# A graph layer on one core: dense attention weights as relu(A*B - 1), written to PSUM by ScalarE, and rows left unscaled

## The chip, the core and the metric

The program runs on one core of a Trainium2 chip. A core has five engines that run their own instruction streams and meet at semaphores: PE (TensorE, matrix multiplications), DVE (VectorE), ACT (ScalarE), POOL (GpSimd, which here issues the gathers) and SP (SyncE, which issues the other DMAs). PSUM is the memory that PE writes to, in eight banks; SBUF is the large on-chip memory. The metric is the device time of one execution in microseconds (us); smaller is better.

## What is computed

The input is a graph of 6250 nodes with 128 features each and 100000 edges `src -> dst`, the edges sorted by `dst`. Low node numbers receive many more edges than high ones.

```python
hs, hd = h[src], h[dst]; e = concat([hs, hd], axis=1)
a_k   = exp(relu(e @ W_att_k + b_att_k))                 # three heads
att_k = segment_sum(a_k, dst)
avg_a = (a1 / att1[dst] + a2 / att2[dst] + a3 / att3[dst]) / 3.0
m     = avg_a * relu(relu(relu(hs @ W1 + b1) @ W2 + b2) @ W3 + b3)
deg   = segment_sum(1, dst)
h_neigh = segment_sum(m, dst) / max(deg, 1)
ref   = relu(concat([h, h_neigh]) @ W_c1 + b_c1) @ W_c2 + b_c2
out   = layernorm(x + ref)
```

The logit of an edge is a sum of a part of its source and a part of its target. With A the exponential of the source's part and B that of the target's (bias included), the factor of a head is `exp(relu(p + q)) = max(A*B, 1)`.

## The kernel before

The program first computes for all nodes, in blocks of 128, their message row and the logit parts, and stores rows of 131 values (128 of the message, 3 logits) in a table in HBM, `message_table`. Then comes the pass over the edges, `edge_pass`.

Edges are taken in groups of 256 (two tiles of 128). The 94 groups with the lowest targets, which all lie in the first 384 nodes, are the hot groups: their edges are not gathered. They are counted into a dense matrix `counts` of 6250 sources by 384 targets (steps 0 to 24), and later the messages of all sources, 49 blocks of 128, are multiplied with dense weights. That is the hot stage: block b is made in step 27 + b, so it fills the steps 27 to 75. The remaining 297 groups are cut into 126 units (four groups each up to unit 23, two after it), one unit a step. POOL gathers a unit's rows by indirect DMA, one for each tile of 128 edges (four a unit from unit 24 on; L1247), into a ring of 12 places. A place comes free when PE has used it, which is what `s_sum` tells.

What a step i does on each engine, in the order of its stream, with the names that the texts use:

- DVE: in the hot stage `hot_weights(b, 0)` (L1765); `logits_of(i + 1)`: a reduction (L1859) and the addition of the gathered logits (L1865), which is the instruction that waits for the gathers of unit i + 1; `weights(i + 1)`: a clamp of the exponentials (L1885) and the product with the one-hot mask (L1890), whose width grows with the unit, 384 elements for 32 columns up to 576 for 48; `hot_weights(b, 1)`, `hot_weights(b, 2)` (L1765); `add_sums(i - 1)`, two additions to the accumulator (L1907); then steps of the finals.
- ACT: `mask_copy(i + 1)` (L1604), `exps(i + 1)` (L1564), finals, `one_hot(i + 3)` (L1554 and L1556), and in the hot stage `scale_rows(b)`: three copies of the block's 129 columns, each times A of one head (L1543).
- PE: `add_edges(i)` (L1434 and L1440), `edge_q(i + 2)` (L1386), in the hot stage `hot_edges(b - 1)`, nine products of 129 columns (L1473, each shown as two instructions in the profile), then finals (L904 and others).

The weights of a head in the hot stage before: `hot_weights` takes `max(B, 1/A)` of the 384 targets (`hot_b` holds B on all lanes, `inverse` holds 1/A), times the counts, and `scale_rows` puts the missing factor A on the rows. Both are in SBUF and neither waits for the other; only PE waits for both.

After the hot stage (`hot_end`, step 77) the hot sums are added, and the finals begin: eleven chunks of four blocks of nodes and three small ones, each in eight steps, spread over the remaining steps to 125, and a tail after the last unit. The order of every stream is written out by hand in the loops over i, and each engine works its stream in order.

## Time and profile before

| | us |
|---|---|
| median of 3 runs (784.7 to 786.55) | 785.11 |
| the profiled execution | 788.37 |
| its span | 784.4 |
| PE busy | 635.0 (81%) |
| DVE busy | 562.6 (72%) |
| ACT busy | 460.2 (59%) |
| POOL busy | 573.6 (73%) |

The span goes from the first to the last instruction of the profiled execution; its own time is 4.0 us longer. Busy shares are means over stages with different limits. The views used below are the chain of waits (what released what, followed back from the end), the waits by engine and line, the timeline, windows (busy time in stretches) and the groups of instructions by shape.

### The profile page before, as it was taken

How to read it: one execution, taken by the hardware profiler on the slowest of the kernel's cores; microseconds unless marked ns; L12 is line 12 of the kernel's file. 1: busy time of each engine (PE TensorE's matmuls, PEld its weight loads, DVE VectorE, ACT ScalarE, POOL GpSimd, SP SyncE). 2: the span in 40 equal slices, each digit the busy share in tenths (PEclk: the TensorE clock that was granted, in tenths of full speed). 3: DMA queues.
4: the chain of work that ended last, by engine and by line, in shares of the span. 5: the costliest groups of instructions: out<-in, count | busy, mean ns of one | idle time of the engine just before them, and what ended most of it. 6: DMA issues, size and time to landing. Idle time of an engine off the chain costs nothing.

```text
span 784.4 us, 17056 instructions
## 1 busy us (share of the span) xinstructions
PE 635.0 (81%) x5157; PEld 519.2 (66%) x5157; DVE 562.6 (72%) x1855; ACT 460.2 (59%) x1109; POOL 573.6 (73%) x604
## 2 busy tenths in 40 slices
PE   9951889988878777999998788797778877878775
PEld 5741657764655456899988677685667766767664
DVE  4884587588888787788886666665567777677566
ACT  6566687578655455667765555553365556566533
POOL 7777777777777677777777777777777777777760
PEclk9985596599778776899999989988798988899698
DMA  7974263334862233333433333324344444444321
GB/s 228 252 195 105 66 101 84 71 85 78 69 83 75 54 96 80 83 87 87 88 83 80 78 74 83 73 64 133 66 107 104 104 111 128 104 117 104 89 59 35
DMA packets 83313, 75.69 MB, mean 96 GB/s; under 512 B 35064, under 2 KB 66720, under 8 KB 83216
## 3 DMA queue, kind: packets, MB, share of 16 engines
q0 software_dynamic: 19008, 39.82, 25.8%
q1 hardware_dynamic: 63920, 34.59, 16.3%
q8 instruction: 44, 0.72, 0.4%
q14 instruction: 53, 0.43, 0.2%
q10 hardware_dynamic: 288, 0.13, 0.1%
HBM read 64.94 MB, written 9.52 MB: 95 GB/s over the span
## 4 chain that ended last, share of the span: by engine, by line
PE 33%; POOL 30%; issue 13%; DVE 11%; ACT 6%; DMA 5%; DVEq 1%; SPq 0%; POOLq 0%; ACTq 0%
POOL work L1247 30%; PE bank L1434 8%; PE bank L1473 7%; PE bank L1457 4%; PE bank L1440 2%; DVE counts L1730 2%; ACT fin L1578 2%; DVE acc L1907 2%; PE bank L592 2%; PE bank L613 2%; PE bank L1391 1%; DVE fin L1717 1%; PE bank L601 1%; DMA message_table<-work 1%; PE bank L1419 1%
## 5 line engine op out<-in xcount | busy, mean ns | idle before, releaser
L1247 POOL DMA_INDIRECT work<-message_table,src_t x554 | 531.6, 960 | 174.2 <-issue 164.9
L1434 PE MATMUL bank<-work 128*128 128x144 f32 (+8 forms) x1188 | 188.5, 314 | 37.9 <-DVE acc L1907 37.8
L1434 PEld LDWEIGHTS bank<-work 128*128 128x128 f32 x1188 | 174.3, 223 | 50.8 <-issue 43.8
L1604 ACT COPY work<-bank 128x192 f32<-128x192 f32 (+7 forms) x126 | 37.4, 297 | 177.4 <-DVE work L1859 176.0
L1473 PE MATMUL bank<-shared,fin 128*128 128x129 f32 (+1 forms) x882 | 115.1, 286 | 0.0
L1907 DVE TENSOR_TENSOR acc<-acc,bank 128x192 f32 (+8 forms) x297 | 89.1, 300 | 27.4 <-issue 3.6
L1473 PEld LDWEIGHTS bank<-shared,fin 128*128 128x128 f32 (+1 forms) x882 | 106.1, 197 | 2.5 <-issue 0.6
L1890 DVE TENSOR_TENSOR work<-bank,work 128x576 f32<-128x576 f32 (+7 forms) x126 | 86.2, 684 | 13.1
L1765 DVE SCALAR_TENSOR_TENSOR fin<-logits_or_x,per_node,counts 128x384 f32<-128x384 f32 (+1 forms) x147 | 85.8, 611 | 1.9 <-PE bank L1473 1.9
L904 PE MATMUL bank<-rest_w,acc 128*128 128x128 f32 x294 | 52.3, 344 | 40.5 <-DVE fin L995 31.0
L904 PEld LDWEIGHTS bank<-rest_w,acc 128*128 128x128 f32 x294 | 46.5, 246 | 43.0 <-DVE fin L995 32.3
L1865 DVE TENSOR_TENSOR work<-work 128x12 f32<-128x12 f32 (+1 forms) x126 | 22.0, 175 | 73.1 <-DMA work<-message_table,src_t 63.8
L1556 ACT ACTIVATE side<-side,one_col 48x512 bf16<-48x512 bf16 x100 | 72.0, 720 | 3.2
L1554 ACT ACTIVATE side<-side,less_col 48x512 bf16<-48x512 bf16 x100 | 70.5, 705 | 0.0
L1457 PE MATMUL bank<-fin 128*128 128x294 bf16 (+2 forms) x188 | 51.4, 416 | 19.4 <-ACT fin L1583 15.8
L1440 PE MATMUL bank<-work 128*4 128x48 f32 (+8 forms) x1188 | 64.8, 204 | 0.0
L1730 DVE TENSOR_TENSOR counts<-counts,bank 128x294 f32 (+2 forms) x94 | 56.3, 599 | 8.2 <-issue 7.3
L1564 ACT ACTIVATE work<-work 128x12 f32<-128x12 f32 (+1 forms) x126 | 27.0, 214 | 55.4 <-DVE work L1865 54.2
L1578 ACT ACTIVATE fin<-fin 128x128 bf16<-128x128 f16 x188 | 59.3, 386 | 0.0
L1386 PE MATMUL bank<-side 48*128 48x57 bf16 (+8 forms) x594 | 37.1, 185 | 24.1 <-DMA side<-logit_parts 20.0
L1440 PEld LDWEIGHTS bank<-work 128*4 128x4 f32 x1188 | 46.0, 89 | 15.9 <-issue 3.4
L1717 DVE TENSOR_SCALAR fin<-fin 128x294 bf16<-128x294 f16 (+2 forms) x188 | 56.4, 343 | 0.0
(162 smaller groups left out, 840.4 us busy)
## 6 DMA issues: line engine op xcount, KB each, us to landing
work<-message_table,src_t POOLq DMA_INDIRECT x554
side<-near_nodes SPq DMA_DIRECT2D x102, 48.0 KB
side<-logit_parts SPq DMA_DIRECT2D x297, 0.8 KB
message_table<-work SPq DMA_DIRECT2D x12, 262.0 KB, 4.7
work<-message_table SPq DMA_DIRECT2D x48, 65.5 KB
work<-in_x_t SPq DMA_DIRECT2D x12, 256.0 KB, 4.9
fin<-in_x SPq DMA_DIRECT2D x11, 256.0 KB, 3.0
logits_or_x<-in_x_t SPq DMA_DIRECT2D x11, 256.0 KB, 3.7
```

The lines of the kernel that those rows point to most:

```text
L904: last = pe.matmul(to[:, k * P:(k + 1) * P], acc[:, k, nodes], wc1[:, 1, :], start=True, stop=True)
L1247: pool.indirect_dma_start(out=rows_of(n)[:, t, :], out_offset=None, in_=table[:, :], in_offset=bass.IndirectOffsetOnAxis(ap=src_t[:, h, g: ...
L1434: pe.matmul(sums[:, at:at + HEADS * w], rows_here[:, t, 0:P], wt_of(i)[:, t, :], start=h == 0, stop=h == TILES - 1)
L1440: last = pe.matmul(sums[SUMS_AT:SUMS_AT + HEADS + 1, at + HEADS * w:at + HEADS * w + w], a_col[:, i % THREE, t, :], mask_of(i)[:, t, :], s ...
L1457: pe.matmul(bank[COUNT_BANKS[g % FOUR]][:, 0:n], hot_lo[:, t % HOT_RING, :], hot_comb[:, t % HOT_RING, 0:n], start=h == 0, stop=h == TILES ...
L1473: last = pe.matmul(bank[SIDE_BANKS[h]][:, k * (P + 1):(k + 1) * (P + 1)], hot_wt[0:m, b % THREE, k, h * P:(h + 1) * P], hot_scaled[0:m, b ...
L1556: act.activation(here, here, ACT.Relu, bias=one_col[0:WIN, 0:1], scale=-1.0).then_inc(s_hot, 1)
L1578: act.activation(hot_lo[:, t % HOT_RING, :], iota16[:, 0:P], ACT.Abs, bias=lo_t[:, g, h:h + 1], scale=-1.0).then_inc(s_lod, 1)
L1730: dve.tensor_tensor(here, here, bank[COUNT_BANKS[g % FOUR]][:, 0:w * n_blocks].rearrange("p (b d) -> p b d", d=w), ALU.add).then_inc(s_cad ...
L1765: dve.scalar_tensor_tensor(hot_wt[0:m, b % THREE, k, :], hot_b[0:m, k, :], inverse[0:m, b, k:k + 1], counts[0:m, b, :], ALU.max, ALU.mult) ...
L1890: dve.tensor_tensor(wt_of(i).rearrange("p t (k w) -> p t k w", w=w), from_q(i)[:, :, PARTS:PARTS + w].unsqueeze(2).to_broadcast([P, n, HEA ...
L1907: dve.tensor_tensor(here, here, sums[:, at:at + (HEADS + 1) * w].rearrange("p (k w) -> p k w", w=w), ALU.add).then_inc(s_acc, 1)
```

## The change

The factor A moves from the rows to the weights. ACT computes `relu(A*B - 1)` for one head and the 384 targets, from `hot_b` with the scale A (`powers`) and the bias -1 (`less_one`), and writes it to one PSUM bank, `EXP_BANK`. DVE reads it there, adds `ok_col` (1 where the logits are within their bounds) and multiplies the counts: `(relu(A*B - 1) + 1) * count = max(A*B, 1) * count`. The rows go to PE as they were loaded, so `scale_rows` goes, and PE and the load of the next block wait for other semaphores. The bank holds one head at a time: ACT waits for DVE's previous `hot_weights` (`s_hw`), and DVE waits for ACT's `hot_excess` (`s_hr`). A reciprocal of 147 columns in step 10 goes too, and two small fills come at the start.

```diff
@@ -198,15 +198,15 @@
-        inverse = per_node_flat[:, 0:n_blocks * HEADS].rearrange("p (b k) -> p b k", k=HEADS)
-        ok_all = per_node_flat[:, n_blocks * HEADS:n_blocks * HEADS + P]
+        ok_all = per_node_flat[:, 0:P]
...
+        less_one = sb("less_one", [P, 1])
...
@@ -255,8 +255,8 @@
-        shared = sb("shared", [P, TWO * HEADS * (P + 1)])
-        hot_scaled = shared[:, :].rearrange("p (j k f) -> p j k f", j=TWO, k=HEADS)
+        SHARED = 5 * P
+        shared = sb("shared", [P, SHARED])
...
+                dve.memset(less_one[:, :], -1.0)
+                dve.memset(shared[:, COLS:SHARED], 0.0)
...
-        BOUND_STEPS, OK_STEPS = 3, 5
+        BOUND_STEPS, OK_STEPS = 3, 4
...
@@ -1275,7 +1277,7 @@
                     def load_block(b):
                         if b >= BLOCKS:
-                            sp.wait_ge(s_hr, HEADS * (b - BLOCKS + 1))
+                            sp.wait_ge(s_hm, b - BLOCKS + 1)
@@ -1466,14 +1468,14 @@
-                        pe.wait_ge(s_hr, HEADS * (b + 1))
+                        rows_here = hot_block[0:m, b % BLOCKS, 0:1 + P]
+                        pe.wait_ge(s_hb[b % BLOCKS], 16 * (b // BLOCKS + 1))
                         for k in range(HEADS):
                             pe.wait_ge(s_hw, HEADS * b + k + 1)
                             for h in range(HOT):
                                 last = pe.matmul(bank[SIDE_BANKS[h]][:, k * (P + 1):(k + 1) * (P + 1)],
                                                  hot_wt[0:m, b % THREE, k, h * P:(h + 1) * P],
-                                                 hot_scaled[0:m, b % TWO, k, :],
-                                                 start=False, stop=b == n_blocks - 1 and k == HEADS - 1)
+                                                 rows_here, start=False, stop=b == n_blocks - 1 and k == HEADS - 1)
@@ -1530,18 +1532,17 @@
-                    def scale_rows(b):
-
-                        m = block_nodes(b)
-                        if b == 0:
+                    def hot_excess(b, k):
+
+                        m, n = block_nodes(b), HEADS * b + k
+                        if n == 0:
+                            act.wait_ge(s_hl, 16 * (HEADS * HOT + 1))
+                            act.wait_ge(s_cadd, n_hot)
                             act.wait_ge(s_ok, OK_STEPS)
-                            act.wait_ge(s_e3, EARLY)
-                        act.wait_ge(s_hb[b % BLOCKS], 16 * (b // BLOCKS + 1))
-                        if b >= TWO:
-                            act.wait_ge(s_hm, b - TWO + 1)
-                        for k in range(HEADS):
-                            act.activation(hot_scaled[0:m, b % TWO, k, :], hot_block[0:m, b % BLOCKS, 0:1 + P], ACT.Copy,
-                                           scale=powers[0:m, b, k:k + 1]).then_inc(s_hr, 1)
+                        else:
+                            act.wait_ge(s_hw, n)
+                        act.activation(bank[EXP_BANK][0:m, 0:hot_nodes], hot_b[0:m, k, :], ACT.Relu, bias=less_one[0:m, 0:1],
+                                       scale=powers[0:m, b, k:k + 1]).then_inc(s_hr, 1)
@@ -1632,6 +1633,8 @@
                     for i in range(n_steps):
+                        if first and 0 <= i - HOT_AT - 1 < n_blocks:
+                            hot_excess(i - HOT_AT - 1, 1)
                         if i + 1 < n_units:
                             mask_copy(i + 1)
                             exps(i + 1)
@@ -1656,7 +1659,9 @@
                         if first and 0 <= i - HOT_AT - 1 < n_blocks:
-                            scale_rows(i - HOT_AT - 1)
+                            hot_excess(i - HOT_AT - 1, 2)
+                        if first and 0 <= i - HOT_AT < n_blocks:
+                            hot_excess(i - HOT_AT, 0)
@@ -1756,14 +1761,11 @@
                     def hot_weights(b, k):
                         m = block_nodes(b)
-                        if b == 0 and k == 0:
-                            dve.wait_ge(s_hl, 16 * (HEADS * HOT + 1))
-                            dve.wait_ge(s_cadd, n_hot)
-                            dve.wait_ge(s_ok, OK_STEPS)
+                        dve.wait_ge(s_hr, HEADS * b + k + 1)
                         if b >= THREE:
                             dve.wait_ge(s_hm, b - THREE + 1)
-                        dve.scalar_tensor_tensor(hot_wt[0:m, b % THREE, k, :], hot_b[0:m, k, :], inverse[0:m, b, k:k + 1],
-                                                 counts[0:m, b, :], ALU.max, ALU.mult).then_inc(s_hw, 1)
+                        dve.scalar_tensor_tensor(hot_wt[0:m, b % THREE, k, :], bank[EXP_BANK][0:m, 0:hot_nodes], ok_col[0:m, 0:1],
+                                                 counts[0:m, b, :], ALU.add, ALU.mult).then_inc(s_hw, 1)
@@ -1779,7 +1781,6 @@
-                        known(dve.reciprocal(inverse, powers[:, :, 0:HEADS]))
```

The line numbers of the changed file are one or two higher than those before. This is the stream of ACT over one hot step (step 27 + b) before. L1543 is `scale_rows`, the others are the edge unit's:

```order
L1604 COPY work<-bank 128x128 [waits s_sum,s_qs]
L1564 ACTIVATE work<-work 128x12 [waits s_a,s_lg]
L1554 ACTIVATE side<-side,less_col 48x512 [waits s_near5]
L1556 ACTIVATE side<-side,one_col 48x512 [waits s_gap]
L1543 ACTIVATE shared<-work,powers 128x129 [waits s_hm,s_hb1]
L1543 ACTIVATE shared<-work,powers 128x129 x2
```

And the same with the change, where L1544 is `hot_excess`; the three that stand together are head 2 of this step's block, head 0 of the next block, and, first in the next step, head 1 of that block:

```order
L1605 COPY work<-bank 128x128 [waits s_sum,s_qs]
L1565 ACTIVATE work<-work 128x12 [waits s_a,s_lg]
L1555 ACTIVATE side<-side,less_col 48x512 [waits s_near2]
L1557 ACTIVATE side<-side,one_col 48x512 [waits s_gap]
L1544 ACTIVATE bank<-logits_or_x,less_one,powers 128x384 [waits s_hw] x3
```

The three copies behind the one-hots are gone; three wider instructions stand in their place, each waiting for DVE, and the third stands ahead of the next unit's copy and exponential.

DVE's stream over one hot step before, from head 0's weights to the two additions:

```order
L1765 SCALAR_TENSOR_TENSOR fin<-logits_or_x,per_node,counts 128x384 [waits s_hm]
L1859 TENSOR_REDUCE work<-bank 128x12 [waits s_q]
L1865 TENSOR_TENSOR work<-work 128x12 [waits s_qs,s_gath8]
L1885 TENSOR_SCALAR work<-work 128x4x3 [waits s_sum,s_exp]
L1890 TENSOR_TENSOR work<-bank,work 128x384 [waits s_a,s_mcopy]
L1765 SCALAR_TENSOR_TENSOR fin<-logits_or_x,per_node,counts 128x384 [waits s_hm] x2
L1907 ISA [waits s_acc,s_sum]
L1907 TENSOR_TENSOR acc<-acc,bank 128x4x32
```

And with the change:

```order
L1767 SCALAR_TENSOR_TENSOR fin<-bank,ok_col,counts 128x384 [waits s_hm,s_hr]
L1860 TENSOR_REDUCE work<-bank 128x12 [waits s_q]
L1866 TENSOR_TENSOR work<-work 128x12 [waits s_qs,s_gath8]
L1886 TENSOR_SCALAR work<-work 128x4x3 [waits s_sum,s_exp]
L1891 TENSOR_TENSOR work<-bank,work 128x384 [waits s_a,s_mcopy]
L1767 SCALAR_TENSOR_TENSOR fin<-bank,ok_col,counts 128x384 [waits s_hm,s_hr] x2
L1908 ISA [waits s_acc,s_sum]
L1908 TENSOR_TENSOR acc<-acc,bank 128x4x32
```

No instruction of DVE moved; each of the three hot products now reads PSUM and waits for ACT (`s_hr`) besides.

## Rows read from the trace of the kernel before

**Rows 1.** The chain of waits by line, stretch 306 to 410 us, then 410 to 784 us.

```profile
by line: PE bank L1473 51.1%; PE bank L1434 23.8%; PE bank L1440 8.3%; PE bank L1386 4.7%; PE bank L1467 4.0%; POOL work L1247 2.2%; issue 1.5%; DVE work L1890 0.9%; DVE acc L1907 0.9%; DVE fin L1765 0.8%; DVEq L1226 0.5%; ACT work L1564 0.
...
by line: POOL work L1247 63.2%; issue 22.3%; DMA work<-message_table,src_t 2.3%; PE bank L904 1.4%; DVE fin L995 1.3%; PE bank L1434 1.0%; DVE stats L1016 1.0%; DVE acc L1907 0.8%; DVE fin L1012 0.8%; DVE work L1885 0.4%; PE bank L915 0.4%;
```

**Rows 2.** Windows of L1890: stretch, its length, busy (count), granted clock, DMA share, GB/s.

```profile
306.00:410.00 104.00, 15.65 (x27) 0.93 0.39 86
410.00:527.00 117.00, 15.08 (x23) 0.94 0.33 75
```

**Rows 3.** Windows of L1247 (POOL), then the timeline of POOL and of DVE.

```profile
306.00:410.00 104.00, 79.29 (x82) 0.93 0.39 86
...
267.32 0.94 POOL L1247 DMA_INDIRECT work<-message_table,src_t  x1 [0.30 <-issue]
...
306.18 0.17 DVE L1865 TENSOR_TENSOR work<-work 128x12 f32<-128x12 f32 x1
```

**Rows 4.** Waits: DVE from 526 to 784 us, POOL over the span, all from 547 us.

```profile
DVE work L1865 <- DMA work<-message_table,src_t: 35.0, 26, 3.4
...
POOL work L1247 <- PE bank L1440: 7.4, 11, 1.8
...
PE bank L904 <- DVE fin L995: 31.0, 11, 3.9
```

**Rows 5.** Timeline of DVE through one hot step: start us, length us, what ran.

```profile
335.09 0.56 DVE L1890 TENSOR_TENSOR work<-bank,work 128x384 f32<-128x384 f32 x1
335.57 1.14 DVE L1765 SCALAR_TENSOR_TENSOR fin<-logits_or_x,per_node,counts 128x384 f32<-128x384 f32 x2
336.62 0.70 DVE L1907 TENSOR_TENSOR acc<-acc,bank 128x128 f32 x2
337.24 0.61 DVE L1765 SCALAR_TENSOR_TENSOR fin<-logits_or_x,per_node,counts 128x384 f32<-128x384 f32 x1
337.76 0.19 DVE L1859 TENSOR_REDUCE work<-bank 128x12 f32<-128x36 f32 x1
338.06 0.17 DVE L1865 TENSOR_TENSOR work<-work 128x12 f32<-128x12 f32 x1
338.51 0.26 DVE L1885 TENSOR_SCALAR work<-work 128x12 f32<-128x12 f32 x1 [0.28 <-ACT work L1564]
338.87 0.56 DVE L1890 TENSOR_TENSOR work<-bank,work 128x384 f32<-128x384 f32 x1
```

**Rows 6.** Timeline of ACT through the same step.

```profile
337.99 0.27 ACT L1604 COPY work<-bank 128x128 f32<-128x128 f32 x1 [1.04 <-DVE work L1859]
338.26 0.21 ACT L1564 ACTIVATE work<-work 128x12 f32<-128x12 f32 x1
338.38 0.70 ACT L1554 ACTIVATE side<-side,less_col 48x512 bf16<-48x512 bf16 x1
339.12 0.72 ACT L1556 ACTIVATE side<-side,one_col 48x512 bf16<-48x512 bf16 x1
```

**Rows 7.** Groups of ACT by shape: busy us, mean ns of one.

```profile
L1543 ACT ACTIVATE shared<-work,powers 128x129 f32<-128x129 f32 x144 | 46.8, 388 | 3.5 <-PE bank L1473 3.4
L960 ACT ACTIVATE fin<-fin,shift,spread 128x128 f32<-128x128 f32 x47 | 19.3, 479 | 0.5 <-DVE shift L1035 0.5
L940 ACT ACTIVATE fin<-bank,scale 128x128 f32<-128x128 f32 x49 | 15.2, 359 | 13.5 <-PE bank L904 13.4
```

**Rows 8.** Groups of DVE by shape.

```profile
L1765 DVE SCALAR_TENSOR_TENSOR fin<-logits_or_x,per_node,counts 128x384 f32<-128x384 f32 x144 | 84.1, 611 | 1.9 <-PE bank L1473 1.9
L995 DVE SCALAR_TENSOR_TENSOR fin<-bank,scale,fin 128x128 f32<-128x128 f32 x98 | 29.7, 344 | 5.5 <-ACT fin L940 4.6
...
L1890 DVE TENSOR_TENSOR work<-bank,work 128x528 f32<-128x528 f32 x16 | 11.3, 708 | 1.7
...
L1782 DVE RECIPROCAL per_node<-powers 128x147 f32<-128x147 f32 x1 | 1.1, 1075 | 0.0
```

**Rows 9.** Windows of all engines from 547 us: PE, PEld, DVE, ACT, POOL, granted clock.

```profile
547.00:767.00 220.00, 171.59 (x1414) 148.66 (x1414) 151.67 (x557) 118.62 (x292) 163.42 (x173) 0.87 0.40 98
```

More of the change, by code:

```diff
@@ L200, in gnn_program @@
         per_node_flat = per_node[:, :, :].rearrange("p b j -> p (b j)")
-        inverse = per_node_flat[:, 0:n_blocks * HEADS].rearrange("p (b k) -> p b k", k=HEADS)
-        ok_all = per_node_flat[:, n_blocks * HEADS:n_blocks * HEADS + P]
-        assert n_blocks * HEADS + P <= n_blocks * LOGITS
+        ok_all = per_node_flat[:, 0:P]
+        assert P <= n_blocks * LOGITS
         parts = sb("parts", [P, n_blocks + 1, PARTS], bf16)
@@ L853, in gnn_program @@
         n_late = sum(finals[c][1] for c in range(B, LAST + 1))
-        assert n_late * P <= TWO * HEADS * (P + 1)
+        assert n_late * P <= SHARED and COLS <= SHARED
         def x_of(c):
```

## The prediction

> **What bounds the kernel now.** I read the chain of waits first, cut where its character changes. From 306 to 410 us it runs through PE: the hot products L1473 and the edge products L1434. From 410 us to the end it is POOL's gathers, 63% and another 22% of "issue", which is the pause between two gathers [rows 1]. The windows tell how fast the steps go. L1890 runs once a step: 27 steps in the first 104 us, 3.85 us each, and 23 in the next 117 us, 5.09 us each [rows 2]. POOL issued 82 gathers in the first of these, 1.27 us each, so a unit of four costs it 5.07 us [rows 3]. So in the first half of the hot stage the steps run faster than POOL delivers. They can because POOL is ahead: the last gather of unit 27 was issued at 267.32 us and DVE took it up at 306.18 us, 38.9 us later [rows 3]. The steps eat that lead until, near 410 us, they wait for each gather. After the hot stage DVE waits 35.0 us in 26 steps for rows [rows 4]. POOL itself waited for a free place in the ring only 7.4 us in the whole run [rows 4].
>
> So nothing but POOL's issue is the bound over the run, and the hot stage has a reserve of its own. The question is how long a hot step may get before the steps after it cannot make it good.
>
> **The change part by part.** I write H for a hot product of DVE, E for the new ACT instruction, and number both by head.
>
> *H reads PSUM.* Before, H is 384 elements in 0.611 us. L995 is the same kind of instruction with a PSUM operand, 128 elements in 0.344 us [rows 8]. L1890 gives the price of an element: 0.56 us for 384 [rows 5] and 0.708 for 528 [rows 8], 1.04 ns each. From 128 to 384 that is 0.27, and 0.344 + 0.27 = 0.61. So H stays at 0.61 us.
> The Trainium skill, page "VectorE: DVE Perf Modes", section on the TRN2 errata, gives a VectorE instruction a fixed part of 120 cycles with a PSUM source and 58 with an SBUF source. By that each H would be some 65 ns longer, 147 of them 9.5 us, an estimate. The two rows above show no such difference, and I go by them.
>
> *E.* No row has it: ACT, 384 elements from SBUF to PSUM, with a column for the scale and one for the bias. L1543 has one column, 0.388 us for 129 elements [rows 7]; L1554, one column, 0.70 for 512 [rows 6]; so an element costs 0.82 ns. L960 has both columns: 0.479 us for 128 elements [rows 7]. E by L960 is 0.479 + 256 x 0.82 ns = 0.69 us. If the second column cost nothing it would be 0.388 + 255 x 0.82 ns = 0.60 us; if PSUM as a target cost as much as that column, 0.78 us. I take 0.69, since L960 is the row of the same form.
>
> *The step.* Before, H0, H1, H2 waited for nobody, and ACT's three copies lay behind its one-hots, off DVE's path. Now one bank passes back and forth, so every H waits for its E and every E for the H before it. From one H0 to the next:
> - H0 0.61, to ACT 0.03 (L1865 ends at 338.23, L1564 starts at 338.26), E1 0.69.
> - E1 stands in ACT's queue ahead of the mask copy and the exponential of the next unit, for which DVE waits. Back to back, ACT's instructions overlap by 0.09 (L1564 ends at 338.47, L1554 began at 338.38) [rows 6]. So -0.09, copy 0.27 - 0.09, exponential 0.21, back to DVE 0.04 (338.51).
> - L1885 to L1890 0.36, L1890 to H1 0.48 [rows 5]. E1 is long done by then.
> - H1 0.61, 0.03, E2 0.69, 0.04, H2 0.61, 0.03, E0 of the next block 0.69, 0.04. ACT's two one-hots, about 1.46 together [rows 6], lie beside L1885 and L1890 and are over before E2. The two additions L1907, 0.70 [rows 5], lie beside E0.
>
> The sum is 5.25 us for units 32 columns wide. DVE's step before was 338.87 - 335.09 = 3.78 us [rows 5]. For 44 columns L1890 is 0.15 longer [rows 8] and the mask copy 0.04; over the stage (14 steps at 32 columns, 16 at 36, 16 at 40, 3 at 44) that adds 0.07. So 5.32 us a step, 49 steps, 261 us. Before, 50 steps took 221 us [rows 2], 49 of them 217. The steps reach the end of the hot stage 44 us later.
>
> *POOL.* It is not slowed. Twelve places at 5.07 us are 61 us of lead at most. It has 38.9 at the start and gains 0.25 a step, 12 in all: 51, so the ring does not fill. It goes on at its own pace and is some 47 us ahead when the hot stage ends.
>
> *What comes back afterwards.* From there the rows lie ready, so DVE's waits for gathers go: 35.0 us [rows 4]. That is the most that can come back. PE is the reason for less. From 547 us it was busy 171.6 of 220 us, and waited 31.0 us at L904 for DVE's L995, a dependence inside the finals [rows 4, 9]. If these waits stay, PE has only 220 - 171.6 - 31.0 = 17 us to give. I take the middle of 17 and 35, 26 us, because part of the L904 waits comes from DVE standing at a gather itself.
>
> *Small edits.* The reciprocal, 1.1 us of DVE once [rows 8], goes from step 10; it is on the path, because now the steps and not POOL set the end from step 0 on: -1 us. The two fills at the start lie beside the first loads: 0, at most 0.3. The load of a hot block now waits for PE instead of ACT. SP issues it four steps ahead of its use, and behind it on SP stand the loads of near nodes and logit parts, three steps or more ahead of theirs: 0. PE now waits for the loaded block, which is there, and its step is 3.85 us at most [rows 2], below 5.3, so the hot products are hidden: 0, where before they were the bound. The freed copies of ACT, three of 0.39, count for nothing, since ACT was not on the path.
>
> **Sum.** 44 - 26 - 1 = +17 us. On the profiled execution, 788.4 us with a span of 784.4, that is 805 us. The median of the runs is 3.3 us below the profiled one: 785.1 + 17 = 802 us.
>
> **Rivals.**
> A, the forecast: hot steps of 5.2 to 5.4 us, part of the loss comes back, 795 to 808 us.
> B, little comes back: the finals are bound by PE and by the hand-over L995 to L904, only PE's 17 us or fewer return. 785 + 44 - 17 - 1 = 811, with 9 us back 819. For it: 23 of the 49 steps after the hot stage already found their rows landed. Against it: 35 us of waiting in the other 26.
> C, POOL's lead covers it, and the time is not slower. It needs E near 0.60 us and all waits returned: 5.32 - 3 x 0.09 = 5.05 us a step, 30 us late, less than 35, so the units catch up with POOL before the end and POOL sets it as before: 785 - 1 = 784. It decides from 4.42 + 35/49 = 5.13 us a step downwards. For it: L940, which reads PSUM, is 0.03 shorter than L1543 from SBUF [rows 7], and PSUM as a target might save the same. Against it: L960 has E's form.
> The Trainium skill, "ScalarE: Activation LUTs", section on what each stage is for, says that ScalarE writes faster to PSUM than to SBUF. No row here has such a write. With L940's 0.03 as its size it would give 3 x 49 x 0.03 = 4 us back, 798 us.
> D, the hand-over costs more: E at 0.78 us, or a hop of 0.1 instead of 0.035. Either adds some 0.25 us a step, 5.6 us, 13 us more over the stage: 815 us. Over 5.44 us a step POOL would meet a full ring too, which costs nothing more while the units trail it. For it: no row shows ACT and DVE alternate on one bank. Against it: the hops in rows 5 and 6 are 0.03 and 0.04.
>
> **How the numbers follow.** A 0.50, B 0.22, D 0.14, C 0.11, anything else 0.03. The single time is A's, 802 us. The unknowns are E (0.60 to 0.78, 30 to 57 us late) and the return (17 to 35): from C's 784 to 785 + 57 - 17 = 825. Leaving out a tenth at each side: 787 to 820 us. A difference below 0.3%, 2.4 us, can't be told from none here. C gives mostly "same": faster 0.03, same 0.08, slower 0.89.
>
> **What the next profile would show.** L1891 (the old L1890) every 5.2 to 5.4 us from step 28 on, evenly, with no change near 410 us; E at 0.69 us and H at 0.61; DVE waiting for ACT L1544 twice a step, about 0.7 us each, some 70 us in all, and PE idle over a quarter of the hot stage; no wait for gathers in the hot stage and hardly any after it, where the chain of waits goes through PE and DVE to the end, not through POOL; POOL done near 765 us as before, the units some 20 us behind it. I am wrong if the step is under 5.13 us, if POOL waits at its ring in the hot stage, or if DVE waits for gathers again before the end, which would mean that it all came back.

## The result and the profile after

| | before | changed |
|---|---|---|
| median of 6 runs, us | 783.71 (781.25 to 786.55) | 801.13 (794.97 to 807.31) |
| ratio, 95% interval | 1 | 1.0208 (1.0147 to 1.027) |
| profiled execution, us | 788.37 | 794.97 |
| its span, us | 784.4 | 791.0 |

The changed kernel is slower by 17.4 us in the medians; forecast were 802.0 and +17. The medians are of all runs, while the ratios, here and below, compare means and leave out the runs that are over 1.5% above the fastest of their kernel (here the one of 807.31 us). The profiled execution of the changed kernel is the fastest of its six runs, and that of the kernel before is longer than any of its six, so the two traces differ by 6.6 us only. "The start" and "The sum" below take this up.

Lines are shifted: L1890, once a step, is now L1891; the hot product H is L1767, the new ACT instruction E is L1544, POOL's gather L1249. First the page of the changed kernel: span, then the busy time of each engine.

```profile
span 791.0 us, 17147 instructions
...
PE 623.0 (79%) x5157; PEld 510.4 (65%) x5157; DVE 566.6 (72%) x1856; ACT 506.4 (64%) x1109; POOL 567.3 (72%) x604
```

ACT is busy for 506.4 us where it was 460.2: E is longer than the copies that it replaces. The other engines hardly differ, and so the page alone doesn't explain 17 us. The windows of L1891 do. First the hot stage, then the time after it (stretch, length, busy and count, granted clock, DMA share, GB/s):

```profile
304.00:563.00 259.00, 30.18 (x49) 0.94 0.36 77
563.00:775.00 212.00, 35.99 (x49) 0.92 0.42 102
```

The same of the kernel before, at its own boundaries:

```profile
309.00:527.00 218.00, 30.18 (x49) 0.94 0.36 80
527.00:768.00 241.00, 35.77 (x49) 0.87 0.41 100
```

49 steps in 259 us are 5.29 us each; before it was 218/49 = 4.45. The stage ends at 563.5 instead of 527.6 and began at 304.1 instead of 309.6, so it lasts 41.4 us longer. Afterwards it is the reverse: 48 steps take 211.2 us (from 563.5 to 774.7) instead of 240.3, 29.1 us back. Last, the start is 5.5 us earlier. 41.4 - 29.1 - 5.5 = 6.8; behind the last step the changed kernel takes 0.2 us less, which makes the 6.6 of the two spans.

The next rows are DVE through one hot step, the counterpart of [rows 5] (start us, length us, what ran, in brackets what it waited for):

```profile
335.55 0.56 DVE L1891 TENSOR_TENSOR work<-bank,work 128x384 f32<-128x384 f32 x1
336.02 0.61 DVE L1767 SCALAR_TENSOR_TENSOR fin<-bank,ok_col,counts 128x384 f32<-128x384 f32 x1
337.38 0.62 DVE L1767 SCALAR_TENSOR_TENSOR fin<-bank,ok_col,counts 128x384 f32<-128x384 f32 x1 [0.74 <-ACT bank L1544]
337.91 0.70 DVE L1908 TENSOR_TENSOR acc<-acc,bank 128x128 f32 x2
338.74 0.62 DVE L1767 SCALAR_TENSOR_TENSOR fin<-bank,ok_col,counts 128x384 f32<-128x384 f32 x1
339.27 0.18 DVE L1860 TENSOR_REDUCE work<-bank 128x12 f32<-128x36 f32 x1
...
340.40 0.17 DVE L1886 TENSOR_SCALAR work<-work 128x12 f32<-128x12 f32 x1 [0.67 <-ACT work L1565]
340.67 0.56 DVE L1891 TENSOR_TENSOR work<-bank,work 128x384 f32<-128x384 f32 x1
```

And ACT through the same step, the counterpart of [rows 6]:

```profile
336.67 0.68 ACT L1544 ACTIVATE bank<-logits_or_x,less_one,powers 128x384 f32<-128x384 f32 x1
338.03 0.68 ACT L1544 ACTIVATE bank<-logits_or_x,less_one,powers 128x384 f32<-128x384 f32 x1 [0.69 <-DVE fin L1767]
339.39 0.67 ACT L1544 ACTIVATE bank<-logits_or_x,less_one,powers 128x384 f32<-128x384 f32 x1 [0.69 <-DVE fin L1767]
340.00 0.26 ACT L1605 COPY work<-bank 128x128 f32<-128x128 f32 x1
340.16 0.20 ACT L1565 ACTIVATE work<-work 128x12 f32<-128x12 f32 x1
```

The two tracks are read against each other. The order of the streams gives the heads: H0 stands ahead of L1860, H1 behind L1891. So these are H1 336.02 to 336.63, E2 from 336.67, H2 at 337.38, E0 of the next block at 338.03, H0 at 338.74, E1 at 339.39. Between the end of one and the start of the other are 0.03 to 0.04 us, and neither engine works on the bank while the other does. Behind E1 stands ACT's copy for the next unit (L1605), behind that the exponential, and DVE waits 0.67 us for it at L1886. The two additions L1908 lie beside E0.

The chain of waits in the hot stage, and after it:

```profile
by line: DVE fin L1767 29.6%; issue 21.9%; ACT bank L1544 21.3%; PE bank L1436 4.5%; PE bank L1476 3.8%; DVE work L1886 3.6%; ACT work L1605 3.6%; DVE acc L1908 2.6%; DVE work L1891 1.5%; PE bank L1442 1.5%; ACT work L1565 1.5%; DVEq L1228 
```

```profile
by line: issue 13.9%; PE bank L906 11.6%; PE bank L1436 9.9%; DVE fin L997 9.0%; DVE acc L1908 6.5%; ACT fin L962 3.6%; DVE stats L1018 3.5%; PE bank L1442 3.5%; DVE fin L1014 2.8%; DVE work L1891 2.6%; DVE work L1886 2.5%; ACT work L1565 2
```

Where [rows 1] had POOL at 63.2% from 410 us on, H and E now take 29.6% and 21.3% of the hot stage, and no gather stands in either list. The groups of E and H (busy us, mean ns of one, idle time ahead) and POOL's gathers from 320 to 500 us:

```profile
L1544 ACT ACTIVATE bank<-logits_or_x,less_one,powers 128x384 f32<-128x384 f32 x144 | 97.1, 675 | 75.7 <-DVE fin L1767 72.8 <-issue 0.7
```

```profile
L1767 DVE SCALAR_TENSOR_TENSOR fin<-bank,ok_col,counts 128x384 f32<-128x384 f32 x144 | 88.5, 614 | 39.8 <-ACT bank L1544 35.9
```

```profile
L1249 POOL DMA_INDIRECT work<-message_table,src_t x145 | 136.9, 944 | 44.2 <-issue 43.0 <-PE bank L1442 1.2
```

And the largest waits of DVE after the hot stage (us, times, mean):

```profile
DVE work L1886 <- ACT work L1565: 15.5, 46, 1.0
DVE work L1860 <- PE bank L1388: 5.8, 11, 0.9
```

The 35.0 us of waiting for gathers [rows 4] are gone altogether: no row of DVE names a DMA after 563 us.

### The profile page after: what moved, and what is told of

Same layout as the page of the kernel before. It is cut to its first block, busy times and chain, and to the rows that moved or that the text cites. A ratio compares the mean times of both kernels' runs of the same rounds, so it can differ in the third digit from the quotient of the medians.

```text
span 791.0 us, 17147 instructions
## 1 busy us (share of the span) xinstructions
PE 623.0 (79%) x5157; PEld 510.4 (65%) x5157; DVE 566.6 (72%) x1856; ACT 506.4 (64%) x1109; POOL 567.3 (72%) x604
## 4 chain that ended last, share of the span: by engine, by line
PE 32%; DVE 30%; ACT 17%; issue 14%; DMA 3%; DVEq 3%; SPq 0%; ACTq 0%; POOLq 0%
DVE fin L1767 10%; PE bank L1436 9%; ACT bank L1544 7%; DVE acc L1908 4%; PE bank L906 3%; PE bank L1459 3%; DVE fin L997 3%; PE bank L1442 3%; DVE work L1886 2%; DVE work L1891 2%; ACT fin L1579 2%; PE bank L594 2%; PE bank L615 2%; DVE counts L1735 2%; PE bank L1476 2%
## 5 line engine op out<-in xcount | busy, mean ns | idle before, releaser
L1249 POOL DMA_INDIRECT work<-message_table,src_t x554 | 525.8, 949 | 170.1 <-issue 166.4
L1436 PE MATMUL bank<-work 128*128 128x144 f32 (+8 forms) x1188 | 185.4, 310 | 71.7 <-DVE acc L1908 71.6
L1436 PEld LDWEIGHTS bank<-work 128*128 128x128 f32 x1188 | 170.1, 219 | 86.4 <-issue 84.9
L1544 ACT ACTIVATE bank<-logits_or_x,less_one,powers 128x384 f32<-128x384 f32 (+1 forms) x147 | 99.2, 675 | 77.3 <-DVE fin L1767 74.4
L1476 PE MATMUL bank<-work,fin 128*128 128x129 f32 (+1 forms) x882 | 120.5, 295 | 0.0
L1767 DVE SCALAR_TENSOR_TENSOR fin<-bank,ok_col,counts 128x384 f32<-128x384 f32 (+1 forms) x147 | 90.3, 614 | 40.6 <-ACT bank L1544 36.6
L1476 PEld LDWEIGHTS bank<-work,fin 128*128 128x128 f32 (+1 forms) x882 | 111.1, 205 | 2.2
L1908 DVE TENSOR_TENSOR acc<-acc,bank 128x192 f32 (+8 forms) x297 | 89.2, 300 | 32.3 <-issue 8.7
L1605 ACT COPY work<-bank 128x192 f32<-128x192 f32 (+7 forms) x126 | 37.0, 294 | 113.8 <-DVE work L1860 113.7
L1891 DVE TENSOR_TENSOR work<-bank,work 128x576 f32<-128x576 f32 (+7 forms) x126 | 86.2, 684 | 13.5 <-DVE work L1886 0.5
L906 PE MATMUL bank<-rest_w,acc 128*128 128x128 f32 x294 | 45.7, 314 | 28.4 <-DVE fin L997 26.0
L1886 DVE TENSOR_SCALAR work<-work 128x12 f32<-128x12 f32 (+1 forms) x126 | 24.8, 197 | 53.4 <-ACT work L1565 45.1
L906 PEld LDWEIGHTS bank<-rest_w,acc 128*128 128x128 f32 x294 | 40.4, 217 | 30.6 <-DVE fin L997 27.2
L1388 PE MATMUL bank<-side 48*128 48x57 bf16 (+8 forms) x594 | 37.1, 185 | 24.3 <-DMA side<-logit_parts 20.3
```

What stands on the lines that cost most here:

```text
L906: last = pe.matmul(to[:, k * P:(k + 1) * P], acc[:, k, nodes], wc1[:, 1, :], start=True, stop=True)
L1249: pool.indirect_dma_start(out=rows_of(n)[:, t, :], out_offset=None, in_=table[:, :], in_offset=bass.IndirectOffsetOnAxis(ap=src_t[:, h, g: ...
L1436: pe.matmul(sums[:, at:at + HEADS * w], rows_here[:, t, 0:P], wt_of(i)[:, t, :], start=h == 0, stop=h == TILES - 1)
L1476: last = pe.matmul(bank[SIDE_BANKS[h]][:, k * (P + 1):(k + 1) * (P + 1)], hot_wt[0:m, b % THREE, k, h * P:(h + 1) * P], rows_here, start=F ...
L1544: act.activation(bank[EXP_BANK][0:m, 0:hot_nodes], hot_b[0:m, k, :], ACT.Relu, bias=less_one[0:m, 0:1], scale=powers[0:m, b, k:k + 1]).the ...
L1767: dve.scalar_tensor_tensor(hot_wt[0:m, b % THREE, k, :], bank[EXP_BANK][0:m, 0:hot_nodes], ok_col[0:m, 0:1], counts[0:m, b, :], ALU.add, A ...
```

## The experiments

The theory on record: DVE and ACT alternate on one bank, so a hot step lasts 5.3 us; POOL's lead covers steps up to 5.13 us; beyond that the rest is lost. Rivals: the loss is instruction time (PSUM at either end), or POOL or PE is slowed by what the change touches. Hot steps are given as the mean of 49, from L1891's windows (L1890's counterpart in each), and each is of one profiled execution.

### e1_excess_late

```
 in ACT's loop, per step
-   hot_excess(b, 1)
    mask_copy(i + 1)
    exps(i + 1)
+   hot_excess(b, 1)
```

> The changed kernel with one move in ACT's stream: the excess of head 1 stands behind the next unit's mask copy and exponential instead of ahead of them. Theory (the hot step is the chain through one bank and ACT's queue): the exponential is ready 0.6 us earlier and so is head 1's product, but then the two one-hots (1.44 us) and head 1's excess keep ACT until 3.1 us after H0, where head 2's excess starts, as late as before (3.06). So the step stays at 5.1 to 5.2 us for 32 columns and the time stays within 3 us of the changed kernel, near 801 us. Rival (the price is only that the exponential is late): the step falls by 0.6 to about 4.5 us, the units are 29 us less late, and the time is that of the kernel before, 784 us.

Measured 799.45 us, 1.0207 (1.0167 to 1.0248). The exponential's wait is gone, but DVE waits longer for the bank instead; one of these waits in full:

```profile
340.44 0.62 DVE L1767 SCALAR_TENSOR_TENSOR fin<-bank,ok_col,counts 128x384 f32<-128x384 f32 x1 [1.05 <-ACT bank L1544]
```

This is H2, waiting for E2. There are 49 such waits, 53.5 us in all, where the changed kernel had 36.5. H1 comes sooner, on average 2.11 us after H0 instead of 2.52, but H2 comes 1.70 us after H1 instead of 1.35, since E2 stands behind the one-hots and E1 and starts, in the step shown, 0.36 us after H1's end instead of 0.04. The step is 5.24 us, hardly shorter. Taking E1 out of the exponential's way alone moves the wait and doesn't remove it.

### e2_excess_between

```
 e1, and
-   hot_excess(b, 2)      # behind both one-hots
 in one_hot, between its Abs and its Relu:
+   hot_excess(b, 2)
```

> As e1_excess_late, and head 2's excess moved between the two one-hots of ACT. Theory: head 2's excess starts when H1 is done, 2.76 us after H0; the step is 4.83 us for 32 columns, 4.9 on average. The units are 24 us late at the end of the hot stage instead of 42, which the later steps return (29 us came back in the changed kernel), so POOL sets the end again: 778 to 788 us. In the changed kernel POOL took 5.0 us a unit in the hot stage against 5.1 before, so it may end some us below the kernel before. Rival (PSUM or the hand-over itself is slow, not the order): 795 us or more.

Measured 780.67 us, ratio 0.9955 (0.9938 to 0.9971): 3.1 us below the median of the kernel before beside it (783.75; 3.5 by the ratio), 18.8 below e1, and 20 below the changed kernel. The same instructions on the same bank; only the place of two of them in ACT's queue differs from the changed kernel, and of one, E2, from e1. ACT in this kernel, E2 between the two one-hots:

```profile
335.86 0.71 ACT L1555 ACTIVATE side<-side,less_col 48x512 bf16<-48x512 bf16 x1
336.83 0.68 ACT L1544 ACTIVATE bank<-logits_or_x,less_one,powers 128x384 f32<-128x384 f32 x1 [0.26 <-DVE fin L1767]
337.44 0.71 ACT L1559 ACTIVATE side<-side,one_col 48x512 bf16<-48x512 bf16 x1
338.19 0.67 ACT L1544 ACTIVATE bank<-logits_or_x,less_one,powers 128x384 f32<-128x384 f32 x1
```

ACT is through with the first one-hot and waits 0.26 us for H1; E2 then starts 0.04 us after H1's end, and the second one-hot lies beside H2. So H1 comes early, as in e1 (2.16 us after H0 on average), and H2 is not held up (1.35 us after H1). From H2 to H0 it is 1.42 us in all three kernels. The window of L1891 in the hot stage (242 us for 49 steps, 4.94 us; at 32 columns most steps take 4.74, expected 4.83), and the chain from 410 us on:

```profile
302.00:544.00 242.00, 30.10 (x49) 0.97 0.35 79
```

```profile
by line: POOL work L1249 29.8%; issue 19.5%; DVE fin L1767 13.4%; ACT bank L1544 9.5%; DVE work L1886 2.8%; DVE fin L997 2.3%; DVE acc L1908 2.3%; ACT work L1567 2.1%; DVE work L1866 1.8%; PE bank L1436 1.6%; DVE work L1860 1.2%; DVE work L
```

POOL is back in the chain with 29.8%, though H and E keep 13.4% and 9.5%: steps and gathers now bound the run nearly together. So the alternation costs little if ACT does its other work in the gaps. The loss follows the order of the hand-over, which is what the theory says and what no rival with dearer instructions can explain, since they are the same ones.

### e3_sbuf_one

```
-   act.activation(bank[EXP_BANK][0:m, 0:hot_nodes], ...
+   act.activation(shared[0:m, 0:hot_nodes], ...        # H reads it there
```

> The changed kernel with the excess written to one SBUF buffer instead of the PSUM bank; order and waits as in the changed kernel. Theory (one buffer passed back and forth is the price, not where it lies): E 0.69 instead of 0.675 us, H 0.61, step 5.15 to 5.2 us for 32 columns, time 800 to 806 us. Rival (the PSUM bank costs): the step falls by 0.2 us or more and the time by 8 us or more. It also shows whether POOL's unit goes back from 5.0 to 5.1 us in the hot stage when DVE reads both operands from SBUF.

Measured 798.57 us (six runs, 793.93 to 924.25), 1.0171 (1.0145 to 1.0198), without the runs of 807.03 and 924.25 us; just below the range of the theory. The profiled execution is the one of 807.03 us. Step 5.34 us, at 32 columns mostly 5.19. E written to SBUF instead:

```profile
L1545 ACT ACTIVATE shared<-logits_or_x,less_one,powers 128x384 f32<-128x384 f32 x144 | 101.8, 707 | 75.0 <-DVE fin L1768 72.4 <-issue 0.2
```

707 ns against 675 to the bank, so PSUM as a target saves 32 ns. It isn't PSUM that makes the change slow; one SBUF buffer is as slow.

### e4_sbuf_two

```
+   excess = shared, two buffers; E and H of number n use n % 2
-   act.wait_ge(s_hw, n)
+   if n >= 2: act.wait_ge(s_hw, n - 1)
```

> The changed kernel with the excess in two SBUF buffers in turn, so that ACT may work one head ahead. Theory: the chain through the buffer is cut; DVE's own work (3.8 us) and ACT's (3.5) set the step with one stall of DVE behind the one-hots, 4.0 to 4.5 us; the units are no later than before the change at the end of the hot stage, the end is POOL's again: 782 to 786 us. Rival (ACT's 0.9 us more work a step is the price): the step stays over 5 us and the time over 795 us.

Measured 783.72 us, 1.0007 (0.9982 to 1.0032): the whole loss is gone. Step 4.53 us, just over the forecast. ACT runs its three back to back, and DVE waits for gathers again after the hot stage:

```profile
336.99 2.08 ACT L1546 ACTIVATE shared<-logits_or_x,less_one,powers 128x384 f32<-128x384 f32 x3
```

```profile
DVE work L1868 <- DMA work<-message_table,src_t: 25.7, 21, 3.0
```

Against e3 the second buffer is the only change, with its wait. 5.34 to 4.53 us a step, 14.9 us in the medians. That the loss comes from the single buffer, and not from E's work on ACT or from H's new operands, is thereby shown.

### The kernel before, with longer steps: e5 to e12

The next question is the knee: does the length of a hot step alone decide, without the hand-over between ACT and DVE? To the kernel before, one idle product is added ahead of H for heads 1 and 2 (e5, e10, e12) or for all three (e6, e9, e11); it goes to a spare tile that nothing reads.

```
 hot_weights, kernel before, for k >= 1 (or k >= 0)
+   dve.scalar_tensor_tensor(spare[0:m, :], bank[EXP_BANK][0:m, 0:hot_nodes],
+                            ok_col[0:m, 0:1], counts[0:m, b, :], ALU.add, ALU.mult)
```

In e7 the three extra products read SBUF (hot_b and inverse, ALU.max) instead; e8 is the changed kernel itself.

> The kernel before with two more products of DVE per hot step, of the shape of the hot products, reading PSUM and writing a spare buffer that nobody reads; the output is unchanged. Theory (only the length of the hot step counts, and up to some 29 to 35 us of delay come back): DVE's step goes from 3.78 by 2 x 0.53 to 4.85 us, 4.9 on average; the units are 49 x 0.46 = 23 us late at the end of the hot stage and POOL still sets the end: 781 to 788 us. Rival (there is no reserve, what the hot stage loses the end loses): 804 to 808 us.

> The kernel before with three more such products per hot step: DVE's step 5.4 us, 5.45 on average, no hand-over between ACT and DVE in it. Theory: the units are 49 us late, 29 come back, the time is 800 to 808 us, as long as the changed kernel or a little more although nothing of the change is in it. Rival (the changed kernel's loss comes from its PSUM bank, its ACT work or its unscaled rows): below 795 us.

> As e6_before_three_more, but the three more products read the targets' factors from SBUF (as the hot products before do). Theory on POOL (a gather's issue takes longer while DVE reads both operands from SBUF): more gathers above 1 us and POOL's unit in the hot stage 5.2 us or more, against 5.1 before and in e6; the time the same as e6 within 4 us, since the steps and not POOL set the end. Rival (POOL's unit depends on something else): the same share of long gathers in e6 and e7.

> The changed kernel again, beside the others of this job. Theory: 795 to 807 us as before, more spread than the kernel before, since POOL no longer covers what the early stage loses in a stretch at the lower granted clock; hot step 5.1 to 5.3 us, POOL's unit 5.0 us, no wait of DVE for gathers after 563 us. Rival: the spread was the chip's and is now below 3 us.

These four ran where the kernel before took 1016.05 us instead of 784. Medians: e5 1016.49 (ratio 1.005, 1.0 to 1.0101), e6 1018.64 (1.0035, 0.9988 to 1.0082), e7 1012.66 (1.0004, 0.9956 to 1.0052), e8 1015.09 (1.0067, 1.0013 to 1.012). POOL's waits in e8:

```profile
POOL work L1249 <- remote: 116.0, 50, 5.7
POOL work L1249 <- PE bank L1442: 82.2, 32, 6.2
```

E and H have their durations (676 and 615 ns), but the engines stand still for stretches for which nothing in the program is the releaser ("remote"). A hot step lasts 6.2 us in all four and POOL's ring is full (82.2 us of waiting; 3.6 in the changed kernel's first profile). A 2% difference can't be seen there, so the times of these runs don't decide the question, and the expectation of e8 on the spread of the runs stays open as well. What e7 shows on the gathers' issue stands in the last section.

> The kernel of e6_before_three_more again, since the chip of that job took 1016 us for the kernel before. Where the kernel before takes about 784 us: theory (only the length of the hot step counts): hot step 5.45 us on average, units 49 us late at the end of the hot stage, 29 come back, 800 to 808 us. Rival (the changed kernel's loss comes from its bank, its ACT work or its rows): below 795 us.

> The kernel of e5_before_two_more again. Theory: hot step 4.9 us on average, 23 us late at the end of the hot stage, all or nearly all returned, POOL sets the end: 781 to 788 us. Rival (no reserve): 804 us or more.

The same again: before 1016.87, e9 1016.51 (0.9971, 0.9933 to 1.001), e10 1015.57 (0.9973, 0.9936 to 1.0009). Inconclusive.

> The kernel of e6_before_three_more a third time, as two chips so far gave some 1016 us for the kernel before. Where that takes about 784 us: theory (only the length of the hot step counts): hot step 5.45 us on average, 800 to 808 us. Rival (the changed kernel's loss comes from its bank, its ACT work or its rows): below 795 us.

> The kernel of e5_before_two_more a third time. Where the kernel before takes about 784 us: theory: hot step 4.9 us on average, 23 us late at the end of the hot stage, all or nearly all returned, POOL sets the end: 781 to 788 us. Rival (no reserve, what the hot stage loses the end loses): 804 us or more.

Here before took 782.85 and 782.34 us. e11: 803.37 us, 1.0247 (1.0217 to 1.0277). e12: 784.65, 1.0019 (0.9999 to 1.0039). e11's steps, in the hot stage and after it:

```profile
306.00:569.00 263.00, 30.12 (x49) 0.93 0.33 73
569.00:781.00 212.00, 35.72 (x48) 0.92 0.42 106
```

5.38 us each, then 4.42, with no wait for a gather after 569 us; in e12 the step is 4.97 us and DVE waits for gathers again:

```profile
DVE work L1872 <- DMA work<-message_table,src_t: 7.3, 6, 2.2
```

e11 has no hand-over between ACT and DVE, only longer steps, and loses what the change loses. All kernels of the runs without such pauses, in order of the hot step:

| hot step, us | kernel | ratio |
|---|---|---|
| 4.45 | before | 1 |
| 4.53 | e4 | 1.0007 |
| 4.94 | e2 | 0.9955 |
| 4.97 | e12 | 1.0019 |
| 5.24 | e1 | 1.0207 |
| 5.29 | changed | 1.0208 |
| 5.34 | e3 | 1.0171 |
| 5.38 | e11 | 1.0247 |

Up to 4.97 us half a microsecond a step, 25 us over the stage, costs next to nothing; at 5.24 it costs 2%. The knee lies between. If every microsecond beyond it reaches the end, the losses of the last four rows (13 to 20 us, shared out over 49 steps) put it at 4.9 to 5.1 us, an estimate from these ratios and steps.

## Why the prediction was right

**The step.** Forecast 5.32 us (5.25 at 32 columns), measured as means 5.29 and 5.22. Behind this stand two misses that nearly cancel. Most steps at 32 columns take 5.13 us, 0.12 less than the path: 0.08 of it lies between L1885 and L1890, where [rows 5] gave 0.36 us and most steps now have 0.28, and the rest mostly in E. And every eighth step is 0.5 us longer, which the prediction didn't have. The additions start late in it, without a releaser:

```profile
348.88 0.71 DVE L1908 TENSOR_TENSOR acc<-acc,bank 128x128 f32 x2 [0.63 <-issue]
```

Once in eight units `add_sums` loads 16 window positions into registers, which isn't counted as busy; that this is the 0.63 us is inferred from the kernel and not tested. The growth over the widths was right: most steps take 5.13, 5.19, 5.26 and 5.31 us at the four widths, 0.08 on average for the forecast 0.07.

Forecast 44 us late, measured 41.4: 1.3 us because 49 steps now take 259.4 us and not 261, as much because they took 218.0 before and not 217. E was taken as 0.69 us and is 0.675; H 0.61 and is 0.614; hops 0.03 to 0.04 as in [rows 5, 6]. The page "VectorE: DVE Perf Modes" of the Trainium skill, section on the TRN2 errata, would have H some 65 ns longer with a PSUM source, by the estimate in the prediction; 0.614 us against 0.611 from SBUF [rows 8] shows no such difference. The page "ScalarE: Activation LUTs" of the Trainium skill, section on what each stage is for, says that ScalarE writes faster to PSUM: e3 agrees, 675 against 707 ns, and the estimate of 0.03 us from L940 was of the right size.

**What comes back.** Forecast 26 us (17 to 35), measured 29.1. By the same reckoning, against the 240.3 us of this profile of before, e1 gives 25.3, e3 24.3 and e11 28.3. The granted clock goes with it: 0.92 in this stretch in the changed kernel and e11, 0.89 in e1 and e3, 0.87 before. So part of the 29.1 may be the clock, which no experiment held fixed. The step "PE has only 17 us to give if the L904 waits stay" was the lower end, and the waits of PE for L997 (the old L995) did shrink:

```profile
PE bank L906 <- DVE fin L997: 26.0, 10, 3.8
```

26.0 us in 10 waits, 31.0 in 11 before [rows 4]. The steps after the stage are now 4.40 us instead of 5.01, set by PE, the finals and DVE in turn; the list of the chain above has "issue" at 13.9% and no line over 12%.

**The knee.** 5.13 us was worked out from 35 us of waiting over 49 steps, and rival C hung on it. The runs say that there is such a knee, but not that it is there: e1 at 5.24 would then lose 49 x 0.11 = 5 us and the changed kernel 8, and both lost 16 by the ratios. 5.13 counted all the waits as returned, while the prediction's own sum had 26 us return, and 4.42 + 26/49 is 4.95; with the measured 4.45 and 29.1 it is 5.04. Besides, the 35 us were read from an execution 4.7 us above the median of before. Between 4.97 and 5.24 nothing was run. C failed at its condition (the step was 5.29), not at its mechanism; e2 and e12 are C come true.

**The rivals.** B fell: 29 us came back, not 9 to 17. D fell: E is 0.675, a hop 0.03 to 0.04. POOL isn't slowed either: its unit in the hot stage is 5.01 us, before 5.11. D's threshold for a full ring, 5.44 us a step, doesn't follow from the numbers given: (61 - 38.9)/49 + 5.07 is 5.52. It was never reached.

**The start.** Forecast -1 us for the reciprocal, found -5.5 in this pair of profiles, more than an instruction of 1.1 us can give. From 110 to 200 us, before and then changed (PE, PEld, DVE, ACT, POOL, granted clock):

```profile
110.00:200.00 90.00, 78.83 (x596) 56.20 (x595) 70.17 (x227) 65.48 (x170) 68.11 (x72) 0.81 0.39 80
```

```profile
110.00:200.00 90.00, 78.65 (x631) 58.95 (x630) 74.90 (x246) 69.97 (x184) 68.04 (x73) 0.87 0.45 83
```

PE works as long in both (78.8 and 78.7 us) but issues 35 matmuls more in the changed one, since its granted clock averages 0.87 instead of 0.81. In the profile of before the clock is at its lower level (1.2 GHz) for the whole of 125 to 156 us, in the other for 111 to 118 and 142 to 152. The reserve doesn't swallow such a loss, for POOL lost nearly as much: its last gather of unit 27 was issued at 267.32 us before [rows 3] and at 262.37 us now, 4.95 of the 5.5 us. Part of that is waiting for a free place in the ring, here up to 306 us, before and then changed:

```profile
POOL work L1247 <- PE bank L1440: 5.5, 5, 1.8
```

```profile
POOL work L1249 <- PE bank L1442: 1.0, 2, 0.7
```

So where the early steps are late, the ring fills and POOL is late too. That the clock makes them late is argued and not shown; no experiment held it fixed. The spread of the changed kernel's runs (12.3 us, against 5.3 before) is no sign of a lost reserve either: e4 and e12, which wait for gathers at the end, spread over 10.2 us. Whether the -1 is there can't be told beside all this.

**The sum.** Forecast +17, in the medians +17.4. By the terms of the profiles it is 41.4 - 29.1 - 5.5, less. The rest is where the two profiled executions lie among their runs: before's 4.7 us above its median, the changed one's 6.2 below; 6.6 + 4.7 + 6.2 = 17.5. Where a median run of the changed kernel spends these last 6.2 us no trace shows. With 41.4 and 29.1 and the reciprocal's 1 the forecast would have been +11, so some of its closeness to 17.4 is luck.

**What was wrong in the list of signs.** "DVE waiting for ACT L1544 twice a step, some 70 us in all" was wrong, and PE's idle share was overstated. From 306 to 563 us, waits and then busy time:

```profile
ACT bank L1544 <- DVE fin L1767: 73.7, 119, 1.3
...
DVE fin L1767 <- ACT bank L1544: 36.5, 49, 0.7
...
PE bank L1436 <- DVE acc L1908: 58.8, 40, 3.1
```

```profile
306.00:563.00 257.00, 199.30 (x1833) 181.06 (x1834) 163.59 (x437) 176.71 (x338) 194.22 (x207) 0.94 0.36 77
```

DVE waits 36.5 us, once a step, for E2. The second wait is filled: the two additions L1908 (337.91 to 338.61 in the step above) lie beside E0, just as the prediction's path of the step has them, and E1 shows as the wait for the exponential behind it (L1886). So this sign contradicted the path that the sum was made from; the sum holds. PE is busy 199.3 of 257 us, idle 22%, not over a quarter; it waits 58.8 us for DVE's additions at L1436. The third miss is POOL's end, forecast for 765 us "as before":

```profile
751.88 0.94 POOL L1249 DMA_INDIRECT work<-message_table,src_t  x1 [0.30 <-issue]
```

That is its last gather, 10 us before the one of the kernel before (761.89). Half of this, 4.95 us, it had at unit 27 already; most of the rest is its unit, 0.10 us shorter over the hot stage. The units end 23 us behind it. The prediction's "POOL is not slowed" was right but "goes on at its own pace" was not: it went faster. As POOL no longer set the end, this moved nothing here. The signs that held: L1891 at 5.1 to 5.4 us but for every eighth step, with no change near 410, no wait for gathers, a lead of 37.4 us at the start and 49.9 at its height (forecast 51), no wait at the ring in the hot stage beyond the 0.30 us that each gather waits anyway.

## What to carry to other kernels

A prefetching engine that bounds the run leaves its consumers a reserve: work out how long their steps may get before it is spent, and charge a change only for what goes beyond. Count only the waits that will come back: with all of them the prediction had 5.13 us a step, with those that its own sum had return 4.95, and the runs point to 4.9 to 5.1. One buffer handed back and forth between two engines costs the sum of both instructions and both hops at every turn; a second buffer (e4) removes that, and so does other work of the waiting engine put into the gap, which is only a question of order (e2, the fastest version here at 780.67 us).

## What the runs showed that was not expected

**The gathers' issue and where other engines' operands lie.** POOL's group from 320 to 500 us in before and in e3:

```profile
L1247 POOL DMA_INDIRECT work<-message_table,src_t x142 | 137.8, 971 | 43.3 <-issue 42.7 <-PE bank L1440 0.6
```

```profile
L1249 POOL DMA_INDIRECT work<-message_table,src_t x140 | 138.3, 988 | 42.7 <-issue 40.2 <-PE bank L1442 2.4
```

971 and 988 ns against 944 in the changed kernel. Issues of over 1 us: before 28 of 141, e3 43 of 140, e4 18 of 142, e11 50 of 135, e12 25 of 141; in the changed kernel, e1 and e2 not one of 144. The three with none have the excess in the bank, the five others don't, and the changed kernel and e3 differ in nothing else that runs in this stretch; there is one profile of each. e6 and e7 differ only in DVE's three added products: in e6 they read the bank and the counts, in e7 SBUF alone (and take the maximum instead of adding). Their gathers from 420 to 700 us, in executions with pauses, where the hot stage lies later:

```profile
L1249 POOL DMA_INDIRECT work<-message_table,src_t x179 | 183.0, 1022 | 97.9 <-issue 45.0 <-remote 42.5 <-PE bank L1442 10.4
```

```profile
L1249 POOL DMA_INDIRECT work<-message_table,src_t x181 | 193.1, 1067 | 88.1 <-issue 46.6 <-remote 35.4 <-PE bank L1442 6.1
```

Over 1 us are 59 of 178 in e6 (e9, the same kernel: 62 of 180) and 81 of 181 in e7, and none of 182 in e8, the changed kernel again. This is what e7's theory expected: what DVE reads matters, with both operands in SBUF more issues are long. It isn't all, since three added products that read the bank raise the share too: e11 has 50 of 135, before, without them, 28 of 141. Whether ACT's write matters besides wasn't tried. POOL's unit from 320 to 500 us is 5.00 us where no issue is long and 5.08 to 5.34 elsewhere. Where POOL is the bound (e2), this may be the gain that was found: 0.10 us over the 49 units of the hot stage are 5 us, against 3.1 measured. No run separates it from e2's other parts.

**Steps that take POOL's length.** In e2 most steps from 36 columns on take 5.00 us, after 4.74 at 32 columns, and in e12 5.1 us after 4.75, which is POOL's unit in each (5.01 and 5.11), although DVE waits for no gather there. In e2 the clamp L1886 then takes 0.34 us instead of 0.17. Why is open; the two points just below the knee may be shorter steps drawn out to POOL's length.

**Executions in which all engines pause.** In e5 to e10 the same kernels took 1016 us instead of 784, with instructions of the usual length and pauses without a releaser. Their cause is open; what they do to a comparison is shown: a 2% loss could not be seen in them.
